# Handing the high/low split of the q and k projections from VectorE to GpSimd, and tile 0's exponential ahead of the copies

## The reference

```python
def _attention(xq, xkv, wq, wk, wv, wo, bo):
    q = (xq @ wq).reshape(B, S, 16, 64)
    k = (xkv @ wk).reshape(B, T, 16, 64)
    v = (xkv @ wv).reshape(B, T, 16, 64)
    attn = jnp.einsum('bihd,bjhd->bhij', q, k) * 64 ** (-0.5)
    attn = jax.nn.softmax(attn, axis=-1)
    out = jnp.einsum('bhij,bjhd->bihd', attn, v).reshape(B, S, 1024)
    return out @ wo + bo

h = _layernorm(x, ln1_g, ln1_b)
x = _attention(h, h, sa_wq, sa_wk, sa_wv, sa_wo, sa_bo) + x
h = _layernorm(x, ln2_g, ln2_b)
x = _attention(h, cond_emb, ca_wq, ca_wk, ca_wv, ca_wo, ca_bo) + x
h = _layernorm(x, ln3_g, ln3_b)
p = h @ ff_w1 + ff_b1
a, gate = (p[..., :1024], p[..., 1024:])
return a * gelu(gate) @ ff_w2 + ff_b2 + x
```

## Time and profile before

| | us |
|---|---|
| median of 3 runs | 1047.44 |
| lowest and highest | 1045.37, 1049.19 |
| the profiled execution's own time | 1047.77 |
| its span, first to last instruction | 1046.0 |
| VectorE busy | 847.7 (81%) |
| ScalarE busy | 623.6 (60%) |
| GpSimd busy | 298.5 (29%) |

### The profile page before, as it was taken

One profiled execution on the slowest core, in us unless ns is written; L12 is line 12 of the kernel. 1 busy time (PEld: TensorE's weight loads), 2 busy tenths in 40 slices (PEclk: granted clock), 3 DMA queues, 4 the chain that ended last, 5 costly groups with the idle time before them and its releaser, 6 DMA issues.

```text
span 1046.0 us, 29695 instructions
## 1 busy us (share of the span) xinstructions
PE 978.5 (94%) x12770; PEld 737.0 (70%) x12770; DVE 847.7 (81%) x996; ACT 623.6 (60%) x1152; POOL 298.5 (29%) x268
## 2 busy tenths in 40 slices
PE   7999999999989999999999899987999999999998
PEld 6676666666656677666666666665677888888887
DVE  4788899999999878999999899999868898554433
ACT  4756667676666656677666576675755544443322
POOL 5113222332322123434223232311314346701000
PEclk9999999999999999999999999999999999999999
DMA  8896676587565856685776676587210001100000
GB/s 179 223 243 161 139 159 146 127 168 164 122 146 117 172 128 138 130 168 121 154 181 127 128 147 138 130 214 154 47 62 21 2 11 42 51 1 21 22 6 36
DMA packets 191940, 121.45 MB, mean 116 GB/s; under 512 B 142657, under 2 KB 159553, under 8 KB 191425
## 3 DMA queue, kind: packets, MB, share of 16 engines
q1 hardware_dynamic: 191808, 119.55, 52.1%
HBM read 56.60 MB, written 12.58 MB: 66 GB/s over the span
## 4 chain that ended last, share of the span: by engine, by line
PE 53%; issue 20%; DVE 8%; POOL 6%; SPq 5%; ACT 5%; DMA 2%; DVEq 0%; POOLq 0%; ACTq 0%
PE W L644 13%; PE SC L616 9%; PE SC L722 8%; PE W L588 5%; PE W L732 4%; POOL X L482 4%; PE W L598 3%; DVE nmax L1215 3%; PE W L900 3%; SPq L265 3%; PE SC L710 2%; DMA w_raw<-in_L_xattn_sa_wk_dram 2%; SPq L314 2%; ACT OTF L995 2%; PE W L657 1%
## 5 line engine op out<-in xcount | busy, mean ns | idle before, releaser
L980 ACT ACTIVATE PR<-SC,nmax 128x1024 f32<-128x1024 f32 x256 | 287.7, 1128 | 208.0 <-DVE nmax L1215 207.6
L1215 DVE TENSOR_REDUCE nmax<-SC 128x1 f32<-128x1024 f32 x256 | 303.3, 1199 | 37.9 <-PE SC L616 37.4
L1220 DVE STREAM_TRANSPOSE PR<-PR 128x1024 f32<-128x1024 f32 x256 | 314.8, 1235 | 15.1 <-ACT PR L980 5.1
L482 POOL TENSOR_TENSOR X<-f_raw,X 128x512 f32<-128x512 f32 x128 | 162.6, 1288 | 456.1 <-ACT f_raw L1007 456.1
L616 PE MATMUL SC<-QKS 64*128 64x512 f32 x1536 | 235.0, 420 | 25.0 <-ACT PR L980 23.6
L644 PE MATMUL W<-PR,V 32*64 32x256 f32 x8192 | 241.9, 379 | 5.0 <-issue 5.0
L644 PEld LDWEIGHTS W<-PR,V 32*64 32x64 f32 x8192 | 186.1, 132 | 53.9 <-issue 21.8
L616 PEld LDWEIGHTS SC<-QKS 64*128 64x128 f32 x1536 | 128.7, 184 | 111.9 <-ACT PR L980 50.8
L1007 ACT ACTIVATE f_raw<-W,rden 128x256 f32<-128x256 f32 x256 | 102.2, 486 | 0.5 <-POOL X L482 0.3
L1288 DVE SCALAR_TENSOR_TENSOR GU<-SC,b,GU 128x512 f32<-128x512 f32 x32 | 24.0, 750 | 70.3 <-ACT GU L1043 70.3
L1043 ACT ACTIVATE GU<-SC,b 128x512 f32<-128x512 f32 x32 | 22.1, 691 | 85.0 <-PE SC L722 85.0
(11 more groups left out here) (132 smaller groups left out, 1473.5 us busy)
## 6 DMA issues: line engine op xcount, KB each, us to landing
QKS<-QKT SPq DMA_DIRECT2D x192, 256.0 KB, 5.0
V<-scratch_v SPq DMA_DIRECT2D x128, 256.0 KB, 5.0
scratch_v<-VST SPq DMA_DIRECT2D x32, 256.0 KB, 4.7
wo<-in_L_xattn_sa_wo_dram SPq DMA_DIRECT2D x64, 64.0 KB, 3.8
f_raw<-in_L_xattn_ff_w_dram SPq DMA_DIRECT2D x12, 256.0 KB, 2.9
X<-in_x_dram SPq DMA_DIRECT2D x4, 512.0 KB, 4.9
w_raw<-in_L_xattn_sa_wk_dram SPq DMA_DIRECT2D x16, 128.0 KB, 4.3
w_raw<-in_L_xattn_sa_wq_dram SPq DMA_DIRECT2D x16, 128.0 KB, 3.9
```

Source lines behind the costliest of these rows:

```text
L482: nc.gpsimd.tensor_tensor(xs, f_raw[:, k % 2, :], xs, ALU.add).then_inc(p_x, 1)
L980: nc.scalar.activation(PR[:, NT * s + t, :], SC[t % 2][:, :], ACT.Exp, bias=nmax[:, t % 4:t % 4 + 1], accum_out=den[:, s, t:t + 1]).then_i ...
L1215: V.tensor_reduce(nmax[:, t % 4:t % 4 + 1], SC[t % 2][:, :], AX, ALU.max, negate=True).then_inc(d_max, 1)
L1220: V.transpose(tile, tile).then_inc(d_tr, 1)
```

## The change

For the groups from g = 2 on, ScalarE copies the scaled projection whole, in float32, into the slot of the low part. GpSimd then rounds it into the slot of the high part and subtracts that in place in the slot of the low part, at the head of its list for the head. VectorE splits only the groups 0 and 1. ScalarE's copies of tile 0 are moved behind the exponential of tile 0 (ahead of that of tile 1), and the transpose of tile 7 in VectorE's list stands directly behind the row maximum of tile 0. TensorE's first burst waits for ScalarE's copies in place of VectorE's subtractions, and SyncE's `place` for GpSimd's.

```diff
--- before.py
+++ after.py
@@ -148,7 +148,7 @@
         m_qk = [sem("m_qk0"), sem("m_qk1")]; m_q1 = [sem("m_q10"), sem("m_q11")]; m_v = [sem("m_v0"), sem("m_v1")]
         m_vst = [sem(f"m_vst{i}") for i in range(4)]
         p_id = sem("p_id"); p_blk = sem("p_blk"); p_wh = sem("p_wh")
-        p_w = [sem("p_wq"), sem("p_wk")]; p_wv = sem("p_wv"); p_f = sem("p_f")
+        p_w = [sem("p_wq"), sem("p_wk")]; p_wv = sem("p_wv"); p_qkv = sem("p_qkv"); p_f = sem("p_f")
         p_xb = sem("p_xb"); p_cn = sem("p_cn"); p_x = sem("p_x"); p_cb = sem("p_cb")
         s_pre = sem("s_pre"); a_pre = sem("a_pre"); a_cnd = sem("a_cnd")
         d_st = sem("d_st"); d_mv = sem("d_mv"); a_sd = sem("a_sd"); d_rs = sem("d_rs"); d_z = sem("d_z")
@@ -399,7 +399,10 @@
                     stored(US - 1)
                     sp.dma_start(CAW[:, :, :], ca_wo.rearrange("(n p) d -> p n d", p=P)).then_inc(m_cao, 16)
                 if p + 1 < GS:
-                    sp.wait_ge(d_qkv, NQ * (p + 2))
+                    if p == 0:
+                        sp.wait_ge(d_qkv, 2 * NQ)
+                    else:
+                        sp.wait_ge(p_qkv, NQ * p)
                     sp.wait_ge(s_sc, 2 * NT * (h + 1))
                     place(p + 1, 0)
                 if p > 0:
@@ -459,6 +462,14 @@
                     pool.wait_ge(s_qkv, NQ * g - 2 * m)
                 split(w_raw[:, m, :, :], w_s[0][:, m, :, :], w_s[1][:, m, :, :]).then_inc(p_w[m], 1)
 
+            def split_qkv(g, n):
+
+                kind, half = proj_of(g, n)
+                m, cols = 2 * "qk".index(kind), slice(half * BANK, (half + 1) * BANK)
+                hi, lo = QKTs[g % 2][:, m, cols], QKTs[g % 2][:, m + 1, cols]
+                pool.wait_ge(a_qkv, NQ * g + n + 1)
+                split(lo.bitcast(F32), hi, lo).then_inc(p_qkv, 1)
+
             def split_v(u):
                 pool.wait_ge(m_wv, 16 * (u + 1))
                 if u > 0:
@@ -504,6 +515,9 @@
                 add_bias(1 + n // 4, n // 2 % 2, by_tile(n), p_cb)
 
             for h in range(HS):
+                for g, n, _ in proj_before(h, 0):
+                    if g > 1:
+                        split_qkv(g, n)
                 g = h // 2 + 2
                 if g == NP + 1:
                     if h % 2:
@@ -628,7 +642,9 @@
                     pe.wait_ge(m_v[s], 64 * (h // 2 + 1))
                     if h > 0:
                         pe.wait_ge(a_op, 4 * h)
-                    pe.wait_ge(d_qkv, ISSUED[h + 1])
+                    if h == 0:
+                        pe.wait_ge(d_qkv, 2 * NQ)
+                    pe.wait_ge(a_qkv, ISSUED[h + 1])
                     pe.wait_ge(a_v, V_ISSUED[h + 1])
                     if h in (NH - 4, NH - 3):
                         pe.wait_ge(d_hl, 4 + 2 * (h - NH + 5))
@@ -948,10 +964,12 @@
                 nc.scalar.activation(sd[:, cols], mv[:, cols, 1], ACT.Sqrt, bias=EPS).then_inc(signal, 1)
 
             def split_qkv(g, n, bank):
+
                 kind, half = proj_of(g, n)
+                m, cols = 2 * "qk".index(kind), slice(half * BANK, (half + 1) * BANK)
+                to = QKTs[g % 2][:, m, cols] if g < 2 else QKTs[g % 2][:, m + 1, cols].bitcast(F32)
                 act.wait_ge(s_qkv, NQ * g + n + 1)
-                nc.scalar.mul(QKTs[g % 2][:, 2 * "qk".index(kind), half * BANK:(half + 1) * BANK], bank,
-                              SCALE if kind == "q" else 1.0).then_inc(a_qkv, 1)
+                nc.scalar.mul(to, bank, SCALE if kind == "q" else 1.0).then_inc(a_qkv, 1)
 
             def evict_v(u, i, bank):
                 act.wait_ge(s_v, 4 * u + i + 1)
@@ -1077,7 +1095,8 @@
                     elif t == 0 and h > 1:
                         scale_out(h - 2, 2)
                         scale_out(h - 2, 3)
-                    for g, n, bank in proj_before(h, t):
+
+                    for g, n, bank in proj_before(h, 0) if t == 1 else proj_before(h, t) if t > 1 else []:
                         if n == 0 and g > 1:
                             for s in range(2):
                                 act.wait_ge(m_qk[s], 64 * (g - 1))
@@ -1313,9 +1332,12 @@
                     if h > 0 and t == 3:
                         turn(h, 2)
                     rowmax(h, t)
+                    if h > 0 and t == 0:
+                        turn(h - 1, NT - 1)
                     for g, n, bank in proj_before(h, t):
-                        split_qkv(g, n, W[:, bank, :])
-                    if (t > 0 or h > 0) and not (t == 3 and h > 0 or t == 5 and summing):
+                        if g < 2:
+                            split_qkv(g, n, W[:, bank, :])
+                    if t > 0 and not (t == 3 and h > 0 or t == 5 and summing):
                         turn(*divmod(NT * h + t - 1, NT))
                     if t == LAST_BURST and summing:
                         turn(h, t)
```

## The result

The changed kernel took 1038.71 us (median of 6 runs, 1035.82 to 1042.56), the kernel before on the same chip 1048.12 (6 runs, 1045.37 to 1050.47): a ratio of 0.9909, with a 95% interval of 0.989 to 0.9929. A second set, of the same file (e1_again), gave 1037.32 against 1048.57, a ratio of 0.9904 (0.988 to 0.9927). So the change saves 9.4 us by the first set and 11.3 us by the second, where the sum in the prediction was 7.0. Both intervals leave out 1, and at their lower ends the saving is 7.4 and 7.7 us. It is a gain, and somewhat more than the reasons given pay for. Most of what follows is about that surplus.

A forecast was written before the change was run, and what follows sets the result against it. TensorE's chain was taken to set ordinary heads' 22.02 us, VectorE only heads where it is late. Terms 1.7 + 1.2 + 1.15 + 1.6 + 1.5 - 0.15 = 7.0 us off 1047.44 gave 1040.4 us, range 1035.5 to 1046.0.

The forecast's parts named there:

- The ordinary head: Summing heads without late VectorE: stay at 22.0 us, gain 0; VectorE's idle before the addition grows from 0.16 to some 1 us.
- Head 29: VectorE sets its end; 2.25 us freed, less perhaps 0.6 for contention: 1.6 us gained, bounds 0.9 and 2.25.
- Heads 12 to 16: Head 12 gains 1.5 us; heads 13 to 16 lose 0.15 us, as the first burst may wait in 13.
- Head 12: TensorE idled 2.00 us before tile 4's scores; VectorE's 2.19 us come off, less contention: 1.5 us, bounds 0.9 and 2.19.
- TensorE's stops: Unexplained stops inside the bursts, 5.0 us in all; may shift by 3 us either way, no term in the sum.
- Part 4: SyncE's `place` starts when GpSimd is done, 4 us later in ordinary odd heads, with room enough: cost 0.
- Part 2: ScalarE's tile 0 exponential begins 0.96 us earlier, ahead of the copies; worth 0 in head 17, counts where TensorE idled.
- The bounds: Terms at their worst give -2.5 us, 1045; at their best some -10 us, 1037.5.
- the rule on contention: VectorE and GpSimd instructions may exclude each other; each pair could lose up to 1.28 us, making the sum 6.0 us.
- The row with 0.62 us: Centring of two pieces took 1.32 us beside GpSimd's subtraction, 0.70 alone; by this measure of contention the sum is 7.0.
- VectorE's busy time: Over the whole kernel: falls by 28 x 1.29 = 36 us, to 812.
- The spare time: Head 18's scores: `place` starts at 439.5, the fourth DMA lands near 447.5, 1 us before it is needed.

The follow-up runs named there:

- the two VectorE experiments: One more VectorE maximum per head (0.643 us, 31 in all), added to the kernel before: 1057.8 us; added to the kernel after: 1038.55 us.
- e1_order: Kernel before with the reordering alone (tile 0's exponential ahead of the copies, tile 7's transpose moved), VectorE keeping its subtractions: 1048.82 us, ratio 1.0009.
- e2_before_late: Kernel before with one more wait on SyncE, so that the projection transfers (`place`) start some 4 us later: 1043.92 us, ratio 0.9961.
- e4_half: Kernel before with 32 one-column matmuls added at the start, shifting TensorE's code by half an instruction packet: 1056.47 us, ratio 1.0067.
- e3_double: Kernel after with one more GpSimd 128x512 multiplication, on data of its own, ahead of every split: 1041.21 us, ratio 0.9935.
- e3_centre: Kernel after with GpSimd's splits of head 12 held back until VectorE's centrings there are done: 1036.84 us, ratio 0.9902.
- e2_before_dve: Kernel before with one more VectorE maximum over a constant tile per head, behind tile 7's transpose: 1057.8 us, ratio 1.0096.
- e2_after_dve: Kernel after with one more VectorE maximum over a constant tile per head, behind tile 7's transpose: 1038.55 us, ratio 0.9909.
- e3_shift: Kernel before with 64 one-column matmuls added at the start, a whole instruction packet of TensorE's code: 1072.87 us, ratio 1.0237.

## Why the prediction was right, and where it wasn't

The time came inside the range, on the side forecast, 1.7 us under the figure.

**The ordinary head.** Right: 22.00 to 22.03 us, 0.90 us of idle time where I said some 1 us, and the two VectorE experiments show the bound where the prediction put it, 10 us against none for the same added instruction.

**The terms.** Between the profiled executions:

```
head      9     26    10    11    27    28     29    12 to 16
forecast  0.86  0.86  0.4   0.4   0.4   1.15   1.6   1.35
profiles  0.88  0.88  0.36  0.21  0.49  1.26   1.93  3.85
```

The seven heads on the left come to 6.0 us where 5.7 were forecast; that part of the sum is right in kind and size. Head 29 got more, since the splits met its centring for only 0.2 us (0.93 us in place of 0.70), where I had taken 0.6 off. Heads 12 to 16 are off, and not through VectorE: e1_order, with the old division of work, took 123.54 us there in place of 125.70, e2_before_late 122.09, and e4_half, the kernel before with its code moved, 120.60, less than the kernel after. Two stops of before (0.79 and 1.49 us) lie in them, and the clock's fall in head 12.

**Head 12** was hit by luck. From its first scores to those of tile 7 it went from 23.86 to 22.06 us, 1.80 less, where the prediction had 1.5. Tile 4's scores did start 0.86 us earlier, but behind the burst TensorE waited 0.75 us longer for ScalarE's copy to OTF (1.21 in place of 0.46). What shortened the head is that the clock stayed up in the burst between the two, 1.69 us. In e4_half, where VectorE keeps its subtractions and the clock didn't fall there either, the same stretch takes 22.44 us. That puts some 1.4 of the 1.80 us on the clock and 0.4 on the change of work. The clock had no term in the sum. That it stayed up because TensorE waited less is not shown: in e3_double it stayed up behind an idle time of 2.63 us.

**The step that was mis-sized most** is the one on TensorE's stops. I put them down as something that may shift by 3 us either way, at zero in the sum. They do have a sign here. Before has 5.0 us of them in its bursts, and the later start of `place`, which Part 4 had at no cost, is what acts on them: alone it is worth 3.9 us (0.9961, interval 0.9946 to 0.9976). So the measured gain holds some 4 us for which the sum had no term. From the whole difference of 9.4 to 11.3 us that leaves 5.5 to 7.4 for the work taken off VectorE and the order, against the 7.0 summed; the two need not add up exactly. The start and heads 30 to 32 gave back 0.84 and 0.93 us: a stop of 0.98 us in head 1's second burst, and the lower clock in head 30.

**The order.** Part 2 gave the exponential's move a share of its own in heads 12, 28 and 29. Alone it has none (1.0009); with the subtractions gone, it has 1.3 us in 28 and 29.

**The bounds.** The terms' own bounds add up to 3.5 us at the worst and 13.8 at the best; the prediction has -2.5 and some -10 without the working. Its 6.0 us by the rule on contention has none either. Neither decides whether the measured time lies inside the range.

**Contention.** The row with 0.62 us was the wrong measure. The pairs lost 1.25 us (1.95 - 0.70) and 0.7 us in head 12, and 0.2 in head 29. The second pair is no new loss, though: it is the one that took 1.32 us before as well. The Trainium skill's rule ("SBUF — State Buffer", "Who interferes with whom"), that one of the two may be shut out for a whole instruction, is the better fit to the first: 1.25 us beside a GpSimd addition of 1.29. The trace agrees: of the first pair one instruction took 1.33 us and the other 0.69, where alone they take some 0.4, and in e3_double, with two long GpSimd instructions beside it, they took 1.33 and 1.36. By e3_centre the splits can be blamed for 0.7 us of the second pair and some 0.3 of the first (1.65 there).

**VectorE's busy time** fell by 25.5 us and not by 36. Added up one by one, the 56 subtractions had 38.5 us. Row maxima grew by 2.8 us (1199 to 1210 ns in the mean), the centring of `X` by 1.3, a subtraction behind the attention by 1.0, the rest by 0.5: 32.9 less. The other 7.4 us are overlap: a row can begin some 0.1 us before the one above has ended, busy time counts that once, and with fewer rows that follow directly on each other there is less of it (48.0 us in place of 55.4).

**SyncE.** `place` of head 17 started at 433.38, which is 439.4 on the time axis of before (436.78 against 442.84 at the addition): 439.5 was forecast. The spare time was 1.96 us, not 1.

## What to carry to other kernels

Count the excess of each repeat over the ordinary one, and cost a change in those repeats; VectorE's 81% of busy time promised a gain in all of them, and only the heads in which VectorE was late gave one. Then test slack by adding work, not by reading the last wait: 20 us of added VectorE time cost 10 us in one kernel and none in the other. Read the granted clock of a stretch before its gain is put down to the work in it: one burst of 3.71 us took 5.40 at 0.50. And look where TensorE idles for "issue" in long runs of small instructions: if the idle time ends 2 to 3 us behind a packet of the instruction queue, when transfers start and how many instructions stand ahead of the loop are worth microseconds, and any change that alters either will seem to gain or lose them.

## What the runs showed of the hardware

TensorE's code comes in packets of 16,384 bytes, some 8.3 us apart in this loop. With the DMA engines loaded, a packet's boundary stopped TensorE for 0.3 to 2.3 us (2.31 in e2_before_dve, 2.12 in e2_after_dve), always at the same place modulo 256 of its instructions and never where the data transfers kept the DMA engines busy for under 86% of the time between TensorE's entry into a block and the next packet; half a packet of code, put ahead, moved all such stops. An fp32 matmul with one column took two passes with its 128 x 128 weights, 112 ns apart at the full clock and 213 ns at 0.50. The granted clock stood at 0.50 for 3.4 us in head 12 of the kernel before, behind 2.00 us of idle time, and for 23.9 us in e3_shift, where it fell during one-column matmuls. VectorE's centring of 2 x (128 x 256) took 0.68 to 0.70 us alone and up to 2.61 us beside GpSimd's tensor_tensor, while its 256 transposes kept their 1235 ns beside the same instructions.
